# The last pair's MLP as two single visits, and matmuls without use while the visit pipeline fills

## The chip, the core and the metric

The kernel runs on one core of one Trainium2 chip. The core has five engines with queues of their own: TensorE (PE, with its weight loads shown apart as PEld), VectorE (DVE), ScalarE (ACT), GpSimd (POOL) and SyncE (SP), which here only starts DMAs. The metric is the device time in microseconds (us) of one execution, as the median of several runs.

## The reference

A batch of 8 sequences of 128 tokens with 144 channels goes through four layers.

```python
# layer 0: rotation in a subspace of 64 dimensions
U, _ = jnp.linalg.qr(P)                      # P is 144 x 64
R = expm(skew(silu(cond) @ W.T + b))         # one 64 x 64 rotation per sequence
z = einsum('btn,nd->btd', x, U)
x = x + einsum('btd,nd->btn', z @ R - z, U)
# layers 1 to 3: transformer blocks with modulation from cond, 16 heads of 9
h = norm(x) * (1 + scale_msa) + shift_msa
x = x + gate_msa * attention(h)              # softmax(q k^T / 3) v, then a projection
h = norm(x) * (1 + scale_mlp) + shift_mlp
x = x + gate_mlp * (gelu(h @ W_fc1 + b) @ W_fc2 + b)     # 144 -> 576 -> 144
```

The third block uses a root-mean-square norm and also normalises q and k; the first two use layer norm.

## The kernel before, in words

Until about 113 us the kernel builds the rotation (a QR by hand on DVE, the matrix exponential on PE) and loads all weights. `WARM_AT` (line 90, used in line 1066) puts 24 matmuls without use, of 512 columns each, between steps of the QR. `rotated` (line 1586) then adds the rotation to `x` in four parts on DVE.

From there on the work is cut into 24 *visits*: visit v is sequence v % 8 in block v // 8. A visit is normalised (`variances`, `normalise`, with the power -1/2 on POOL), its 16 last channels are split on POOL into bf16 parts (`tail_parts`, line 523, six small steps that wait for one another), it is transposed on PE (`h_turn`), scaled on ACT (`h_out`), multiplied with the qkv weights (`qkv`), split into bf16 parts (`first` on ACT, `split` on DVE), and transposed, half by PE (`parts_turn`) and half by two DMA transposes that SP starts (line 370). Then come the scores, their maxima on DVE (`maxima`, `max_parts`, `max_turn`, `max_out`), the scores again transposed, the exponentials, the product with v, the projection (`proj`), its gate (`gated`) and `attention_add` on POOL. `scores(v, 0)` takes heads that PE has transposed; `scores(v, 2)` waits for the DMA transposes.

The MLP runs in *pairs* of visits, m = v // 2, so 12 pairs: `second_input`, `second_deviation`, `second_normal`, `second_half_tail`, `h2_turn`, `h2_out`, `fc1` in three steps through PSUM banks 5, 0, 5, `gelu` after each step, `fc2` in two halves, `mlp_out` on DVE, `mlp_add` on POOL.

The order is written out by hand: every engine walks over the same slots (`for slot in range(-2, VISITS + 6)`) and each slot lists which visit or pair does what on that engine. `visit_at(work, v)` calls the work if v is a visit; `pair_at(work, slot, lag)` calls it for the pair m with slot = 2 m + lag. Even and odd slots differ, and in the third block some have an order of their own. Each engine works through its list strictly in order and waits at semaphores. `refill(bank, ...)` waits until the last reader of a PSUM bank is done. ACT must load a table to go between exp and gelu (`bring_table`); `to_exp` and `to_gelu` do that with an activation of one column. The last pair (m = 11, visits 22 and 23) has its norm in slot 25 and the rest of its MLP in slots 26 to 28, when there is no attention left. SP stores `x` in four transfers of two sequences, each after its pair's `mlp_add`.

Of the kernel before, what the change touches and what calls it, by code (L numbers as in the profile page):

```python
# [26 lines left out]
BF16 = mybir.dt.bfloat16  # L27
U32 = mybir.dt.uint32
I32 = mybir.dt.int32
ALU = mybir.AluOpType  # L30
# [3 lines left out]
B, T, C = 8, 128, 144  # L34
# [21 lines left out]
STEPS = LAYERS * B // 2  # L56
LN_EPS = [1e-6, 1e-5, 0.0]
# [6 lines left out]
VISITS = LAYERS * B  # L64

# [49 lines left out]
def program(nc, t, out, spread_mods):  # L115
    ctx = ExitStack()
    with ctx:
# [181 lines left out]
        fc2_full, mlp_ready, mlp_added = sem("fc2_full"), sem("mlp_ready"), sem("mlp_added")  # L299
        stored = sem("stored")  # L300
# [16 lines left out]
        def _(sp):  # L317
# [54 lines left out]
            for pair in range(B // 2):  # L372
                sp.wait_ge(mlp_added, STEPS - B // 2 + pair + 1)
                sp.dma_start(out[:, 2 * pair:2 * pair + 2, :], x[:, 2 * pair:2 * pair + 2, :]).then_inc(stored, 16)
            sp.wait_ge(stored, 16 * (B // 2))
# [3 lines left out]
        FC1_BANKS = (5, 0, 5)  # L379
        ROT_BANKS = (2, 4, 6, 2)  # L380

        def mlp_step(slot, lag):

            m = (slot - lag) // 2
            return m if slot >= lag and (slot - lag) % 2 == 0 and m < STEPS else None
# [6 lines left out]
        def pair_at(work, slot, lag, *args):  # L392

            if mlp_step(slot, lag) is not None:
                work(mlp_step(slot, lag), *args)
# [6 lines left out]
        def _(pool):  # L402
# [160 lines left out]

            def second_half_tail(m, h):
                second_tail(2 * m + h)
# [18 lines left out]
            for slot in range(-2, VISITS + 6):  # L584
                if (slot + 1) // B == 2 and slot % 2 == 0:
                    pair_at(second_half_tail, slot, 4, 1)
                    pair_at(mlp_add, slot, 6)
# [11 lines left out]
                elif slot % 2 == 0:  # L599
                    pair_at(second_half_tail, slot, 4, 1)  # L600
                    pair_at(mlp_add, slot, 6)
# [3 lines left out]
                else:  # L605
# [4 lines left out]
                    pair_at(second_half_tail, slot, 3, 0)  # L610


        @block.scalar
        def _(act):
# [161 lines left out]
            def to_exp(m):  # L776
                if m < STEPS - 1:
                    bring_table(ACT.Exp)
# [16 lines left out]
            def modulated(v, kind):  # L795

                h, l, b = v % 2, v // B, v % B
                out_, at = (hT_t[h][:], 0) if kind == 0 else (mT_t[:, h, :], h * T)
                return a.activation(out_, ps[:, 0, at:at + T], ACT.Identity, bias=mod_t[:, l, 2 * kind, b:b + 1],  # L799
                                    scale=mod_t[:, l, 2 * kind + 1, b:b + 1])  # L800

# [23 lines left out]
            for slot in range(-2, VISITS + 6):  # L825
# [49 lines left out]
                else:  # L875
# [11 lines left out]
                    visit_at(o_out, slot - 1)  # L887


        @block.tensor  # L890
        def _(pe):
# [276 lines left out]

            def parts_turn(v, k):
# [16 lines left out]
            def scores(v, g):  # L1186
                if g == 0:
# [62 lines left out]
            pe.wait_ge(sel_ready, 1)  # L1250
            h_turn(0)
            qkv(0)
            h_turn(1)
            for slot in range(-2, VISITS + 6):
# [60 lines left out]
                else:  # L1315
# [18 lines left out]
                    visit_at(pv, slot - 1, 3)  # L1334


        @block.vector
        def _(dve):
# [394 lines left out]

            def next_input(v):
# [35 lines left out]
            for slot in range(-2, VISITS + 6):  # L1770
                if (slot + 1) // B == 2 and slot % 2 == 0:
                    pair_at(mlp_out, slot, 6)
# [31 lines left out]
                elif slot % 2 == 0:  # L1804
                    pair_at(mlp_out, slot, 6)
# [12 lines left out]
                else:  # L1818
# [13 lines left out]
                    pair_at(second_normal, slot, 3)  # L1832

# [99 lines left out]
```

## Time and profile before

| | |
|---|---|
| median of 3 runs | 399.44 us (399.34 to 399.56) |
| profiled execution, its own time | 396.7 us |
| its span, first to last instruction | 394.9 us |
| busy: PE, DVE, ACT, POOL | 316.3, 297.9, 222.1, 165.1 us |
| chain that ended last | DVE 41%, PE 29%, issue 10%, ACT 6%, DMA 5%, POOL 5% |
| mean granted TensorE clock | 0.900 of full speed |

The profiled execution took 2.7 us less than the median. The page cuts the span into 40 slices of 9.87 us; digits are tenths. Granted clock 0.5 is 1.2 GHz, and 1.0 is 2.4 GHz. The chain is followed back from the last instruction; "issue" in it is time in which nothing that the profile shows was waited for.

### The profile page before, as it was taken

What the parts mean: (1) busy time and instruction counts of PE and PEld (TensorE: products, weight loads), DVE (VectorE), ACT (ScalarE), POOL (GpSimd) and SP (SyncE); (2) the same over time, 40 slices, a digit from 0 to 9 for tenths busy, and PEclk for the clock granted to TensorE, in tenths of its full rate; (3) what the DMA queues carried; (4) which work ended last, traced back from release to release, by engine and by line L of the source; (5) the groups of instructions that cost most, each with busy time, mean ns of one, the idle gap of its engine ahead of it and who ended that gap; (6) DMA issues with size and microseconds to landing.
All of it is one profiled execution on the core that took longest, in us unless ns stands there. A gap on an engine that the chain in (4) does not pass through costs nothing.

```text
span 394.9 us, 10842 instructions
## 1 busy us (share of the span) xinstructions
PE 316.3 (80%) x3516; PEld 215.9 (55%) x3516; DVE 297.9 (75%) x1507; ACT 222.1 (56%) x484; POOL 165.1 (42%) x536
## 2 busy tenths in 40 slices
PE   1979938836565678999999999988898888978935
PEld 1826413631232455777777776756566655756724
DVE  5999999999944778777777877768797888866110
ACT  3244101430023466879797978785868768575721
POOL 5434323656430313535444453535546364613140
PEclk9998556995765699999999999999999999999968
DMA  5797000194001221211121211110022111101000
GB/s 148 202 269 241 6 1 3 31 268 148 1 0 27 28 29 29 42 23 40 23 42 30 30 29 28 29 28 14 16 28 29 29 28 28 30 15 31 17 15 15
DMA packets 36303, 20.43 MB, mean 52 GB/s; under 512 B 27882, under 2 KB 34766, under 8 KB 36120
## 3 DMA queue, kind: packets, MB, share of 16 engines
q1 hardware_dynamic: 36248, 19.75, 21.0%
q8 instruction: 29, 0.48, 0.5%
q14 instruction: 26, 0.21, 0.2%
HBM read 12.82 MB, written 0.62 MB: 34 GB/s over the span
## 4 chain that ended last, share of the span: by engine, by line
DVE 41%; PE 29%; issue 10%; ACT 6%; DMA 5%; POOL 5%; SPq 2%; POOLq 0%; ACTq 0%; DVEq 0%
PE ps L893 23%; DMA skw_r<-brief 5%; DVE nmax L1683 4%; DVE grow L1380 4%; DVE top L1435 3%; DVE trow L1380 3%; DVE beta L1414 2%; DVE den L1420 2%; SPq L370 2%; PE ps L1173 2%; DVE tfac L1428 2%; PE ps L1234 2%; DVE brief L1670 2%; DVE lead L1402 2%; DVE late L1402 2%
## 5 line engine op out<-in xcount | busy, mean ns | idle before, releaser
L1683 DVE TENSOR_REDUCE nmax<-ps 128x4 f32<-128x512 f32 x96 | 62.3, 685 | 28.5 <-PE ps L893 28.3
L438 POOL TENSOR_TENSOR root<-grow,half 32x1 f32<-32x1 f32 x64 | 34.8, 544 | 53.2 <-DVE grow L1380 52.8
L754 ACT ACTIVATE skw_t<-ps 128x512 f32<-128x512 f32 x96 | 54.1, 596 | 5.2 <-PE ps L893 5.1
L893 PE MATMUL ps<-skw_r 54*128 54x128 bf16 x768 | 46.4, 222 | 7.1 <-DMA skw_r<-brief 4.5
L893 PEld LDWEIGHTS ps<-skw_r 54*128 54x128 bf16 x768 | 29.5, 96 | 21.4 <-issue 13.7
L893 PE MATMUL ps<-mT_t,fc1w_t 128*128 128x256 f32 x120 | 39.4, 421 | 2.0 <-ACT mT_t L799 1.6
L893 PE MATMUL ps<-fc2w,skw_r 128*128 128x144 f32 (+1 forms) x240 | 34.6, 292 | 0.6 <-ACT skw_r L786 0.6
L547 POOL TENSOR_TENSOR x<-x,skw_r 128x144 f32<-128x144 f32 x24 | 11.7, 489 | 53.5 <-DVE skw_r L1723 53.5
L893 PEld LDWEIGHTS ps<-fc2w,skw_r 128*128 128x128 f32 (+1 forms) x240 | 31.2, 190 | 3.9 <-issue 2.1
L552 POOL TENSOR_TENSOR rstd<-vare,nhalf 128x1 f32<-128x1 f32 x24 | 13.2, 552 | 45.5 <-DVE vare L1603 30.2
L771 ACT ACT_TABLE_LOAD x23 | 29.5, 1283 | 0.4
L893 PE MATMUL ps<-nmT,sel 64*128 64x128 bf16 x384 | 27.8, 219 | 0.0
L761 ACT ACTIVATE skw_t<-ps 128x512 f32<-128x512 f32 x24 | 14.3, 595 | 23.5 <-PE ps L893 23.5
L893 PE MATMUL ps<-skw_t,brief 128*32 128x128 f32 x512 | 22.1, 280 | 5.5 <-DVE skw_r L1723 4.9
L893 PE MATMUL ps<-qkvw_t,hT_t 128*128 128x432 f32 x48 | 24.9, 604 | 1.0 <-ACT hT_u L807 0.8
L893 PEld LDWEIGHTS ps<-mT_t,fc1w_t 128*128 128x128 f32 x120 | 19.2, 201 | 10.1 <-issue 7.0
L786 ACT ACTIVATE skw_r<-ps 128x512 f32<-128x512 f32 (+1 forms) x36 | 18.5, 522 | 8.7 <-PE ps L893 8.5
L1173 PE MATMUL ps<-identb,brief 128*128 128x128 bf16 x192 | 16.8, 226 | 8.0 <-DVE brief L1672 8.0
L538 POOL TENSOR_TENSOR tail<-ln,gmod 128x16 f32<-128x16 f32 x48 | 11.0, 228 | 25.7 <-DVE ln L1616 21.5
L747 ACT ACTIVATE skw_r<-ps 128x512 bf16<-128x512 bf16 x24 | 14.3, 595 | 9.6 <-PE ps L1173 9.1
L1173 PEld LDWEIGHTS ps<-identb,brief 128*128 128x128 bf16 x192 | 13.2, 101 | 11.4 <-issue 10.5
L893 PEld LDWEIGHTS ps<-nmT,sel 64*128 64x128 bf16 x384 | 19.0, 95 | 0.0
(262 smaller groups left out, 828.5 us busy)
## 6 DMA issues: line engine op xcount, KB each, us to landing
gmod<-spread_mods SPq DMA_DIRECT2D x3, 1408.0 KB, 13.2
adaw_t<-in_ada SPq DMA_DIRECT2D x3, 432.0 KB
tails<-in_tail SPq DMA_DIRECT2D x3, 427.1 KB
skw_t<-in_skw SPq DMA_DIRECT2D x1, 1024.0 KB
fc1w_t<-in_fc SPq DMA_DIRECT2D x3, 320.0 KB
fc2w<-in_fc SPq DMA_DIRECT2D x3, 288.0 KB
skw_r<-brief SPq DMA_TRANSPOSE x48, 2.6
qkvw_t<-in_qkv SPq DMA_DIRECT2D x3, 216.0 KB
```

The source lines that it names most:

```text
L438: g.tensor_tensor(root[:, p, j:j + 1], grow[:, i % 4, 0:1], half[:], ALU.pow).then_inc(root_ready, 1)
L552: g.tensor_tensor(rstd[:, 0, h:h + 1], vare[:, 0, h:h + 1], nhalf[:, 0:1], ALU.pow).then_inc(rstd1, 1)
L747: a.activation(qkT[1][v % 2][:, 0:4, :].rearrange("p k t -> p (k t)"), ps[:, 7, :].bitcast(BF16)[:, 0:4 * T], ACT.Copy).then_inc(kT_ready, 1)
L754: a.activation(prob[g].rearrange("p i t -> p (i t)"), ps[:, 2 + g % 2, :], ACT.Exp, scale=SCALE).then_inc(prob_ready, 1)
L761: a.activation(o_raw[v % 2].rearrange("p g t -> p (g t)"), ps[:, 4, :], ACT.Copy).then_inc(o_raw_ready, 1)
L771: a.activation(table_out[:], half[:], f).then_inc(table_used, 1)
L786: a.activation(hid[0:rows, 2 * r:2 * r + n, :, :].rearrange("p c h t -> p (c h t)"), ps[0:rows, FC1_BANKS[r], 0:n * 2 * T], f).then_inc(hi ...
L893: return pe.matmul(o, lhsT, rhs, start=start, stop=stop, skip_group_check=True)
L1173: i = pe.transpose(o[:, pair * T:(pair + 1) * T], parts[k][v % 2][:, 2 * pair:2 * pair + 2, :].rearrange("p h d -> p (h d)"), identb[:])
L1380: return d.stream_shuffle(out_, rows, [j] * HALF)
L1402: i = d.scalar_tensor_tensor(out=elim[p][:, w], in0=grow[:, (HALF * p + j) % 4, 1:D + 1], scalar=gfac[:, p, j:j + 1], in1=elim[p][:, w], o ...
L1683: d.tensor_reduce(nmax[:, v % 2, first:first + 7:2], ps[:, 6 + g % 2, :].rearrange("p (i t) -> p i t", i=4), AX_X, ALU.max, negate=True).t ...
```

## The change

It has two parts that don't touch.

*The end.* The MLP of visits 22 and 23 is no longer pair 11 but two single visits with functions `last_...`. There are 11 pairs left (`PAIRS`), the slots end at 25, and what the pair 10 would have done in slot 26 (`mlp_out`, `mlp_add`) is called by hand. Visit 22 is normalised in slot 24 on DVE and POOL, visit 23 after slot 25. On PE, after slot 25, come `last_turn(22)`, `last_tail_turn(22)`, `last_fc1_main(22)`, `last_fc1_tail(22)`, `last_turn(23)`, `last_products(22)`, and then visit 23's own steps. Each visit has four PSUM banks (`LAST_BANKS`), so neither waits for the other's. Matmuls of `fc1` now have 128 columns instead of 256, and all first parts of a visit stand ahead of all second parts. `to_exp` is left out after pair 10, and so is the next `to_gelu`. The last `x` addition is done on DVE instead of POOL, and SP stores the two last sequences one by one.

*The start.* `stay_warm(n)` issues n matmuls without use, of 512 columns in bf16, into PSUM bank 5. They stand in the PE list at: 4 before `h_turn(0)`, 6 inside it (between its two transposes), 4 after it, 1 after `qkv(0)`, 11 after `h_turn(1)`; then 6 ahead of `scores(0, 2)` and 6 ahead of `scores(1, 2)`, 6 ahead of `max_turn(0)` and 2 ahead of `max_turn(1)`: 46 in all.

```diff
+PAIRS = STEPS - 1
...
+LAST = VISITS - 2
...
-            for pair in range(B // 2):
+            for pair in range(B // 2 - 1):
                 sp.wait_ge(mlp_added, STEPS - B // 2 + pair + 1)
                 sp.dma_start(out[:, 2 * pair:2 * pair + 2, :], x[:, 2 * pair:2 * pair + 2, :]).then_inc(stored, 16)
-            sp.wait_ge(stored, 16 * (B // 2))
+            for b in range(B - 2, B):
+                sp.wait_ge(last_done, b - B + 3)
+                sp.dma_start(out[:, b:b + 1, :], x[:, b:b + 1, :]).then_inc(stored, 16)
+            sp.wait_ge(stored, 16 * (B // 2 + 1))
...
+        LAST_BANKS = ((1, 6, 7, 2), (0, 3, 4, 5))
...
-            return m if slot >= lag and (slot - lag) % 2 == 0 and m < STEPS else None
+            return m if slot >= lag and (slot - lag) % 2 == 0 and m < PAIRS else None
...
+            def last_deviation(v):
+                h = v % 2
+                pool.wait_ge(last_var, v - LAST + 1)
+                g.tensor_tensor(rstd[:, 1, h:h + 1], vare[:, 1, h:h + 1], nhalf[:, 0:1], ALU.pow).then_inc(last_rstd, 1)
+            def last_parts(v):
+                tail_parts(1, v, (last_ln, v - LAST + 1), (h2T_full, PAIRS), last_tail)
...
-            for slot in range(-2, VISITS + 6):
+            for slot in range(-2, VISITS + 2):
...
-                    pair_at(mlp_add, slot, 6)
+                    pair_at(mlp_add, slot, 6, stop=PAIRS - 1)
...
+                if slot == VISITS:
+                    last_deviation(LAST)
+                    last_parts(LAST)
+            last_deviation(LAST + 1)
+            last_parts(LAST + 1)
+            mlp_add(PAIRS - 1)
...
-                if m < STEPS - 1:
+                if m < PAIRS - 1:
...
+            def last_modulated(v):
+                act.wait_ge(last_turned, v - LAST + 1)
+                act.wait_ge(fc1_full, 3 * PAIRS)
+                modulated(v, 1, LAST_BANKS[v % 2][0], 0).then_inc(last_mod, 1)
+            def last_tail_out(v):
+                act.wait_ge(last_tail_turned, v - LAST + 1)
+                a.activation(mT_u[:, v % 2, :], ps[:, LAST_BANKS[v % 2][1], :].bitcast(BF16)[0:KS, 0:T],
+                             ACT.Copy).then_inc(last_u, 1)
+            def last_gelu(v, r):
+                act.wait_ge(last_fc1, 3 * (v - LAST) + r + 1)
+                act.wait_ge(fc2_full, PAIRS)
+                rows, n = (128, 2) if r < 2 else (64, 1)
+                bank = LAST_BANKS[v % 2][(2, 3, 0)[r]]
+                a.activation(hid[0:rows, 2 * r:2 * r + n, v % 2, :], ps[0:rows, bank, 0:n * T].rearrange("p (c t) -> p c t", t=T),
+                             ACT.Gelu_apprx_tanh).then_inc(last_hid, 1)
...
+            last_modulated(LAST)
+            last_tail_out(LAST)
+            last_gelu(LAST, 0)
+            last_gelu(LAST, 1)
+            last_gelu(LAST, 2)
+            last_modulated(LAST + 1)
+            last_tail_out(LAST + 1)
+            last_gelu(LAST + 1, 0)
+            last_gelu(LAST + 1, 1)
+            last_gelu(LAST + 1, 2)
...
+            def stay_warm(n):
+                for r in range(n):
+                    mm(ps[:, 5, :], identb[:], sel[:, 4 * (r % 4):4 * (r % 4) + 4, :])
...
                 pe.transpose(o[:, 0:T], ln[0][v % 2][:, 0:128], ident[:])
+                if v == 0:
+                    stay_warm(6)
                 pe.wait_ge(tailp_ready, v + 1)
...
+            def last_turn(v):
+                o = refill(LAST_BANKS[v % 2][0], last_mod, v - LAST + 1)
+                pe.wait_ge(v_ready, VISITS)
+                pe.wait_ge(last_ln, v - LAST + 1)
+                pe.transpose(o[:, 0:T], ln[1][v % 2][:, 0:128], ident[:]).then_inc(last_turned, 1)
+            def last_tail_turn(v):
+                o = refill(LAST_BANKS[v % 2][1], last_u, v - LAST + 1)
+                pe.wait_ge(last_tail, v - LAST + 1)
+                turn_parts(o.bitcast(BF16)[0:KS, 0:T], tailp[1][v % 2]).then_inc(last_tail_turned, 1)
+            def last_part(v, c):
+                bank, at = LAST_BANKS[v % 2][(2, 2, 3, 3, 0)[c]], (c % 2) * T
+                return ps[:, bank, at:at + T]
+            def last_fc1_main(v):
+                for bank in LAST_BANKS[v % 2][2:4]:
+                    refill(bank, last_hid, 3 * (v - LAST) + 2)
+                pe.wait_ge(last_mod, v - LAST + 1)
+                for c in range(FFC):
+                    mm(last_part(v, c), fc1w_t[2][:, c * 128:c * 128 + 128], mT_t[:, v % 2, :], c % 2 == 0, False)
+            def last_fc1_tail(v):
+                pe.wait_ge(last_u, v - LAST + 1)
+                for c in range(FFC):
+                    at = 3 * C + c * 128
+                    i = mm(last_part(v, c), tailw[:, 2, at:at + 128], mT_u[:, v % 2, :], False, True)
+                    if c % 2 == 1 or c == FFC - 1:
+                        i.then_inc(last_fc1, 1)
+            def last_products(v):
+                h = v % 2
+                for c in range(FFC):
+                    pe.wait_ge(last_hid, 3 * (v - LAST) + c // 2 + 1)
+                    rows = 128 if c < 4 else 65
+                    i = mm(ps[:, LAST_BANKS[h][1], 0:C], hid[0:rows, c, h, :], fc2w[2][0:rows, c, :], c == 0, c == FFC - 1)
+                i.then_inc(last_fc2, 1)
...
             def scores(v, g):
+                if v < 2:
+                    stay_warm(3 * g)
...
             def max_turn(v):
+                if v < 2:
+                    stay_warm(6 - 4 * v)
...
             pe.wait_ge(sel_ready, 1)
+            pe.wait_ge(rot_read, 2)
+            stay_warm(4)
             h_turn(0)
+            stay_warm(4)
             qkv(0)
+            stay_warm(1)
             h_turn(1)
-            for slot in range(-2, VISITS + 6):
+            stay_warm(11)
+            for slot in range(-2, VISITS + 2):
...
+            last_turn(LAST)
+            last_tail_turn(LAST)
+            last_fc1_main(LAST)
+            last_fc1_tail(LAST)
+            last_turn(LAST + 1)
+            last_products(LAST)
+            last_fc1_main(LAST + 1)
+            last_tail_turn(LAST + 1)
+            last_fc1_tail(LAST + 1)
+            last_products(LAST + 1)
...
+            def last_input(v):
+                dve.wait_ge(att_added, v + 1)
+                variances(1, [v], last_var)
+            def last_normal(v):
+                dve.wait_ge(last_rstd, v - LAST + 1)
+                dve.wait_ge(h2T_full, PAIRS)
+                normalise(1, v, last_ln)
+            def last_out(v):
+                h, b = v % 2, v % B
+                dve.wait_ge(last_fc2, v - LAST + 1)
+                dve.wait_ge(mlp_added, PAIRS)
+                need(did(d.tensor_tensor(mlpd[:, h, :], ps[:, LAST_BANKS[h][1], 0:C], gmod[:, 2, b, C:2 * C], ALU.mult)))
+                d.tensor_tensor(x[:, b, :], x[:, b, :], mlpd[:, h, :], ALU.add).then_inc(last_done, 1)
...
+                if slot == VISITS:
+                    last_input(LAST)
+                    last_normal(LAST)
+            last_input(LAST + 1)
+            mlp_out(PAIRS - 1)
+            last_normal(LAST + 1)
+            last_out(LAST)
+            last_out(LAST + 1)
```

## Rows read from the trace of the kernel before

**Rows 1.** The page: granted clock by slice of 9.87 us, in tenths.
```profile
PEclk9998556995765699999999999999999999999968
```
**Rows 2.** The chain, as pipeline fills: start us, us, what.
```profile
115.98 0.36 PE ps L1116
...
117.18 2.15 PE ps L893 x3
...
122.31 1.01 PE ps L1173 x8
123.32 2.49 PE ps L893 x11
...
127.24 0.63 PE ps L893 x8
...
131.40 1.19 SPq L370
...
132.63 3.31 DMA skw_r<-brief
```
**Rows 3.** By stretch: us, PE busy (instructions), PEclk, DMA share, GB/s.
```profile
114.00:115.00 1.00, 0.30 (x1) 0.83 0.00 0
...
134.00:135.00 1.00, 1.00 (x7) 0.50 0.32 58
```
**Rows 4.** Timeline of PE, the matmuls without use: start us, us, operation.
```profile
91.85 6.53 PE L893 MATMUL ps<-sel,identb 128*128 128x512 bf16 x15 [4.37 <-DVE grow L1380]
99.00 0.82 PE L893 MATMUL ps<-sel,identb 128*128 128x512 bf16 x3 [0.62 <-DVE grow L1380]
```
**Rows 5.** Timeline of PE later, at full clock: the filling's same groups.
```profile
148.98 0.61 PE L1173 MATMUL ps<-identb,brief 128*128 128x128 bf16 x8 [1.06 <-DVE brief L1672]
...
149.42 0.28 PE L1121 MATMUL ps<-ident,ln 128*128 128x128 f32 x1
...
150.95 0.99 PE L893 MATMUL ps<-qkvw_t,hT_t 128*128 128x432 f32 x2
...
151.78 0.35 PE L893 MATMUL ps<-tailw,hT_u 102*128 102x432 bf16 x1
```
**Rows 6.** Timeline, all engines, from the last attention work to the end.
```profile
373.84 1.39 PE L893 MATMUL ps<-fc2w,skw_r 128*128 128x144 f32 x10
...
374.43 0.49 POOL L547 TENSOR_TENSOR x<-x,skw_r 128x144 f32<-128x144 f32 x1 [7.58 <-DVE skw_r L1723]
...
377.53 0.22 POOL L538 TENSOR_TENSOR tail<-ln,gmod 128x16 f32<-128x16 f32 x1 [0.41 <-DVE ln L1619]
...
380.64 0.22 POOL L543 TENSOR_TENSOR tailp<-tail,tailp 128x16 bf16<-128x16 f32 x1
...
391.92 0.79 POOL L570 TENSOR_TENSOR x<-x,skw_r 128x288 f32<-128x288 f32 x1 [10.31 <-DVE skw_r L1731]
```
**Rows 7.** Timeline, one visit's norm alone, and visit 22's attention addition.
```profile
280.13 0.30 DVE L1597 BATCH_NORM_STATS2 st<-x 128x6 f32<-128x144 f32 x1
...
281.76 0.29 DVE L1619 TENSOR_SCALAR ln<-x,rstd 128x144 f32<-128x144 f32 x1 [0.67 <-POOL rstd L552]
...
366.35 0.49 POOL L547 TENSOR_TENSOR x<-x,skw_r 128x144 f32<-128x144 f32 x1
...
370.92 0.26 DVE L1708 RECIPROCAL orec<-ps 128x16 f32<-128x16 f32 x1 [4.70 <-PE ps L1234]
```
**Rows 8.** Timeline, prices of single steps near the end.
```profile
372.11 0.39 ACT L793 ACTIVATE x_t<-ps 128x256 f32<-128x256 f32 x1 [0.21 <-PE ps L1112]
...
374.04 0.31 DVE L1723 TENSOR_TENSOR skw_r<-ps,gmod 128x144 f32<-128x144 f32 x1 [2.52 <-PE ps L893]
...
381.57 0.80 ACT L799 ACTIVATE mT_t<-ps,mod_t 128x128 f32<-128x128 f32 x2
```
**Rows 9.** By stretch, near the end: us, PE busy (instructions), PEclk, DMA share, GB/s.
```profile
377.50:378.00 0.50, 0.40 (x2) 0.50 0.00 0
...
387.50:388.00 0.50, 0.50 (x3) 0.77 0.00 0
```

More of the change, by code:

```diff
@@ L299, in program @@
         fc2_full, mlp_ready, mlp_added = sem("fc2_full"), sem("mlp_ready"), sem("mlp_added")
+        last_var, last_rstd, last_ln, last_tail = sem("last_var"), sem("last_rstd"), sem("last_ln"), sem("last_tail")
+        last_turned, last_mod = sem("last_turned"), sem("last_mod")
+        last_tail_turned, last_u = sem("last_tail_turned"), sem("last_u")
+        last_fc1, last_hid, last_fc2, last_done = sem("last_fc1"), sem("last_hid"), sem("last_fc2"), sem("last_done")
         stored = sem("stored")
@@ L390, in visit_at, with pair_at @@
                 work(v, *args)
-        def pair_at(work, slot, lag, *args):
-            if mlp_step(slot, lag) is not None:
+        def pair_at(work, slot, lag, *args, stop=STEPS):
+            if mlp_step(slot, lag) is not None and mlp_step(slot, lag) < stop:
                 work(mlp_step(slot, lag), *args)
@@ L600, in _ @@
                     pair_at(second_half_tail, slot, 4, 1)
-                    pair_at(mlp_add, slot, 6)
+                    pair_at(mlp_add, slot, 6, stop=PAIRS - 1)
                     visit_at(attention_add, slot - 2)
@@ L793, in o_T, with modulated @@
                 a.activation(oT[v % 2].rearrange("p k t -> p (k t)"), ps[:, 4, 0:2 * T], ACT.Copy).then_inc(oT_ready, 1)
-            def modulated(v, kind):
+            def modulated(v, kind, bank=0, at=None):
                 h, l, b = v % 2, v // B, v % B
-                out_, at = (hT_t[h][:], 0) if kind == 0 else (mT_t[:, h, :], h * T)
-                return a.activation(out_, ps[:, 0, at:at + T], ACT.Identity, bias=mod_t[:, l, 2 * kind, b:b + 1],
+                out_ = hT_t[h][:] if kind == 0 else mT_t[:, h, :]
+                at = h * T * kind if at is None else at
+                return a.activation(out_, ps[:, bank, at:at + T], ACT.Identity, bias=mod_t[:, l, 2 * kind, b:b + 1],
                                     scale=mod_t[:, l, 2 * kind + 1, b:b + 1])
+            def last_modulated(v):
[13 more added lines that the diff above has]
+                             ACT.Gelu_apprx_tanh).then_inc(last_hid, 1)
             def h_out(v):
@@ L1250, in _ @@
             pe.wait_ge(sel_ready, 1)
+            pe.wait_ge(rot_read, 2)
+            stay_warm(4)
             h_turn(0)
+            stay_warm(4)
             qkv(0)
+            stay_warm(1)
             h_turn(1)
-            for slot in range(-2, VISITS + 6):
+            stay_warm(11)
+            for slot in range(-2, VISITS + 2):
                 if (slot + 1) // B == 2 and slot % 2 == 0:
@@ L1768, in second_normal @@
                     normalise(1, v, ln2_ready)
-            for slot in range(-2, VISITS + 6):
+            for slot in range(-2, VISITS + 2):
                 if (slot + 1) // B == 2 and slot % 2 == 0:
-                    pair_at(mlp_out, slot, 6)
+                    pair_at(mlp_out, slot, 6, stop=PAIRS - 1)
                     visit_at(q_out, slot)
@@ L1804, in _ @@
                 elif slot % 2 == 0:
-                    pair_at(mlp_out, slot, 6)
+                    pair_at(mlp_out, slot, 6, stop=PAIRS - 1)
                     visit_at(attended, slot - 2)
```

## The prediction

> **What bounds the kernel now.** First the page: the granted clock by slices shows two stretches of the visit part at less than full speed, the filling of the pipeline after about 113 us and the last three slices [rows 1]. The change touches just these. So two views were read for each: the chain of waits, which says what ends last, and the timeline with the table by stretch, which say what a step costs at either clock.
>
> In the filling no engine is full; the chain goes from one engine to the next: norm, transposes, qkv, split, scores, maxima. Its TensorE pieces are 0.36, 2.15, 1.01, 2.49 and 0.63 us [rows 2], all at 0.5 of the clock: it fell in the microsecond after 114 and was still 0.5 in the one before 135 [rows 3]. Behind that stretch the chain waits for a DMA transpose, 1.19 us on SP and 3.31 us to its landing [rows 2], so what comes later moves rigidly with the start of that DMA.
>
> At the end, attention is over when `attention_add` of visit 23 ends at 374.92 (374.43 + 0.49) [rows 6]. Then the last pair's MLP runs alone: norm of both visits, two bf16 splits on POOL one after the other (377.53 to 380.86), transposes, scaling, fc1, gelu, fc2, gate and the last addition, which ends at 392.71 [rows 6]. That is 17.8 us in which nearly nothing overlaps. The span ends at 394.9, so 2.2 us more for the last store.
>
> **The end, part by part.** Visit 22's attention is added at 366.84 (366.35 + 0.49) [rows 7], 8 us before visit 23's. A single visit's norm takes 1.92 us from its statistics to the end of the normalised tile (280.13 to 282.05) [rows 7]; a split of one visit takes half of 3.33, so 1.7 us [rows 6]. Visit 22 in slot 24 is thus normalised by 368.8 and split by 370.6. I cost it at nothing: TensorE is in pair 10's fc1, attention's end and fc2 until 375.23 (373.84 + 1.39) [rows 6]. The waits that this adds in slot 24: on DVE the next item, `attended(23)`, stands behind `last_normal(22)` and ran at 370.92 [rows 7], 2.1 us after it; on POOL `attention_add(23)` stands behind the split and ran at 374.43, 3.9 us after. Were that cover gone, a late split would push everything after 374.43 one for one.
>
> From 375.23 on, the path in steps; durations are at full clock:
> - transpose of 22: 0.28 [rows 5], ends 375.5; scaling on ACT, half of the 0.80 for two visits [rows 8] and some fixed part, so 0.46: 376.0; with 0.1 for the hand-over 376.1.
> - `last_fc1_main(22)`: no row has f32 matmuls of 128 columns. Nearest are fc2's of 144 columns, ten in 1.39 us [rows 6], so 0.26 to 0.28 for the two records of a chunk. Five chunks are 1.3: 377.4. Bounds: 1.1, and 2.4 at half clock by the ratio below.
> - second parts and the first gelu: 0.4 until ACT begins, 377.8. Two gelus of 256 columns at 0.39 (the copy of that size) [rows 8] and one of 128 columns, taken as 0.3: 378.9. Meanwhile visit 23 has been normalised (374.92 + 1.92 = 376.9) and `last_turn(23)` done; `last_products(22)` follows the gelus and ends at about 379.4.
> - scaling of 23, which ACT has behind 22's gelus: 0.46 and hand-over, 379.4. Five chunks: 380.8. Visit 23's split is done at 378.7, hidden. Its transpose and the copy by ACT stand behind the main part: 0.7, 381.5. Second parts: 381.9. Gelus: 383.0. Last product: 0.5, 383.5.
> - gate 0.31 [rows 8] and the same for the addition on DVE: 384.2.
>
> The last addition ended at 392.71, so this part gives 8.5 us. The table loads that go lay beside POOL's splits and TensorE's first fc1 steps and give nothing. `mlp_add(10)` moves behind the split of 23, to about 379.5, and holds up `last_out(22)` on DVE; the next item there, `last_out(23)`, comes at 383.5, so it costs nothing. SP stores one sequence last instead of two; I take the 2.2 us as before. Bounds of the part: 9.5 if ACT and hand-overs are shorter than taken, 4.8 if all of it ran at half clock (the rival below).
>
> **The start, part by part.** A matmul without use costs 0.435 us at half clock (15 in 6.53), and three issued at once later took 0.82 with the last one's latency in it, which fits 0.22 each [rows 4]. That the clock rises under them is in the same rows. If it stays full from 114 on:
> - the 4 before `h_turn(0)` end at about 114.4, just when its transpose can run. The 6 inside end at about 116.0, when POOL's split ends (115.98 is when the next transpose began) [rows 2]. The 4 after it take 0.9 beside ACT's scaling (116.34 to 117.18). Cost nothing to 0.1.
> - `qkv(0)`: 2.15 becomes 1.18 (150.95 to 152.13) [rows 2, 5]: 1.0 gained.
> - 1 + 11 run beside the split into parts on ACT and DVE, which takes 3.0 us (119.33 to 122.31) [rows 2]; they end about 0.15 after the parts are ready: 0.15 lost.
> - `parts_turn` 1.01 to 0.61 [rows 2, 5], `qkv(1)` 2.15 to 1.18, scores 0.63 to 0.43: 1.5 gained, so maxima start 2.4 earlier. Then `scores(0, 2)` follows them, but it needs the DMA transposes as well. By the chain's own pair, 1.19 + 3.31, they land up to 4.5 after the parts; they would be 0 to 0.5 later than DVE. I take 0.2 lost, the last scores give 0.2 back.
> - the 6 ahead of `scores(0, 2)` and 6 ahead of `max_turn(0)` are 1.3 each, beside maxima that take 1.4 (125.81 to 127.24) [rows 2]: nothing. The 6 ahead of `scores(1, 2)` end with the DMA they wait for: 0.1. The 2 ahead of `max_turn(1)`: 0.43 us of work where TensorE has little time free, 0.15 taken. After that the clock was full before too, so nothing more.
>
> Sum: 1.0 − 0.15 + 1.5 − 0.1 and − 0.4 for small collisions is about 1.8 us. Bounds: 2.6, and −1 if parts of it run at half clock.
>
> **The sum.** 8.5 + 1.8 = 10.3. The profiled execution would go from 396.7 to 386.4, its span from 394.9 to 384.6. The median shown is 2.7 above that execution; I subtract the gain from it: 399.44 − 10.3 = 389.1 us.
>
> **Rivals.**
> - *Clock falls at 114.8 all the same.* Before, TensorE was busy for 0.30 of the microsecond after 114, and the clock fell in it [rows 3]; the change adds four matmuls, 0.9 us, just before. If it falls, the 6 inside `h_turn(0)` take 2.6 instead of 1.3 and hold the second transpose 1.3 back, the 4 after it some 0.4 more, until the added work has raised the clock again; of the later gains what is left leaves about 0.4 for the start: 390.5. For it: that fall. Against it: six more follow almost at once.
> - *Clock falls in the tail.* Ratio 2.15 to 1.18 [rows 2, 5]. All of it at half: each main part of fc1 +1.0, `last_products(22)` +1.2 before TensorE is free for 23, the rest +0.5: 3.7 lost, 392.8; half of it, 391.0. Against: before, TensorE had nothing to do from 375.23 and was at 0.5 only in the stretch from 377.50 [rows 9]; now the hole is 0.6 to 0.9 us. The same row shows the price before: clock back only in the stretch from 387.50.
> - Beside it, a rule: the Trainium skill (TensorE: Matmul & The Clock Gate, Part 4: PE-mode transpose) says that transposes do not count as work for the clock as matmuls do. By that rule the transposes at 375.2 would not help, and this second rival, 391.0, would be likelier; no row here separates the two.
> - *The added matmuls stand in the way (slower).* If the clock does not rise under them, all 46 cost 0.435, not 0.22. By the places above, in half-clock lengths (six are 2.6 from 115.6 on where the transpose wants to start at 116.0, and so on): 2.2 + 0.8 in `h_turn(0)` and behind it, 2.8 for the 11, 1.1, 0.4, 2.4 for the three sixes, 0.5 for the two: 10.2 lost against 8.5 won, 401.1. It decides from 8.5 us on. Against it: [rows 4] show the clock raised by just such matmuls.
> - *The single visits do not overlap as said*, for instance since ACT holds visit 23 back behind 22's gelus for longer: half of the end's gain, 393.4.
>
> **How the numbers follow.** Forecast 389.1: 62%. Fall at 114.8, 390.5: 17%. Fall in the tail, 391.0: 12%. No overlap, 393.4: 5%. Slower, 401.1: 2%. Something in between with no change: 2%. The range reaches up over the tail rival to 392.4, and down by the upper bounds of both parts, 9.5 and 2.6, to 387.3. About 0.2% is what can be told from no change here. Faster 0.96, within 0.02, slower 0.02.
>
> **What would show it.** Right: granted clock near 1.0 without a break from 111 us on; `qkv(0)` at 1.2 us; `last_turn(22)` directly behind the last `fc2`; last addition on DVE about 9.3 us after `attention_add(23)` ends, instead of 17.8. The start is read from where the first DMA transposes of visit 1 begin: 131.40 before, 129.3 to 129.7 after. Wrong: a stretch at 0.5 in either place, fc1 chunks of 128 columns well above 0.28, a transpose or `scores(0, 2)` waiting behind added matmuls, `attended(23)` or `attention_add(23)` late behind visit 22's new steps.

## The result, and the profile after

The changed kernel takes 386.33 us (median of 4; 384.53 to 386.86), against 399.39 for the kernel before: ratio 0.9695, interval 0.9653 to 0.9737. The gain is 13.1 us; the forecast was 10.3, and 386.33 lies under the range's lower end of 387.3. But the profiled executions fell only from 396.7 to 386.9, by 9.8 us. That sum looks nearly right, but the table says otherwise. It cuts the span at the first rotated addition on DVE and at the attention additions on POOL, which this text numbers from 1 to 24 (the 24th is visit 23's). It gives what each stage gained, once from the first profile to the changed kernel's first, and once between the means of three profiles of each kernel (*before*, *e1* and *e16* against *after*, *e4* and *e15*; the runs are told below).

| stage | forecast | first pair, us | means of three, us |
|---|---|---|---|
| start of the span to the first rotated addition | 0 | -0.72 | -0.25 |
| from there to the 4th addition (the filling) | 1.8 | -0.34 | 1.71 (62.29 to 60.58) |
| 4th to 11th addition | 0 | 0.01 | -0.11 |
| 11th to 14th addition | 0 | 1.88 | 1.86 (31.96 to 30.10) |
| 14th to 24th addition | 0 | 0.02 | 0.02 |
| end of the 24th to the end of the last addition | 8.5 | 8.81 | 8.74 (17.72 to 8.98) |
| last addition to the end of the span | 0 | 0.14 | 0.17 |
| sum | 10.3 | 9.8 | 12.1 |

So in the first pair the forecast's 1.8 us of the filling did not come, and 1.9 us came from a stage that the forecast had as rigid. In the later runs, 85 executions of the kernel before spread from 396.1 to 402.0 us, with their median at 398.4: the same code differs by several us from one execution to the next.

The page's clock row of the changed kernel (slices of 9.63 us, tenths), to be held against [rows 1]:

```profile
PEclk9988555568969898999999999999999999999999
```

The last slices are full, and the filling (from the thirteenth slice on) nearly so; the twelfth slice, which ends at 115.5 us, has 0.6. The end, from the timeline of the changed kernel (start us, us, engine, operation):

```profile
372.99 1.39 PE L946 MATMUL ps<-fc2w,skw_r 128*128 128x144 f32 x10
...
373.58 0.49 POOL L557 TENSOR_TENSOR x<-x,skw_r 128x144 f32<-128x144 f32 x1 [3.81 <-DVE skw_r L1840]
...
374.22 0.27 PE L1233 MATMUL ps<-ident,ln 128*128 128x128 f32 x1
...
375.13 1.35 PE L946 MATMUL ps<-mT_t,fc1w_t 128*128 128x128 f32 x10 [0.58 <-ACT mT_t L824]
...
376.63 0.81 ACT L842 ACTIVATE skw_r<-ps 128x256 f32<-128x256 f32 x3 [1.48 <-PE ps L946]
...
378.40 1.28 PE L946 MATMUL ps<-mT_t,fc1w_t 128*128 128x128 f32 x10
...
380.86 1.49 PE L946 MATMUL ps<-fc2w,skw_r 128*128 128x144 f32 x10 [0.31 <-ACT skw_r L842]
...
382.74 0.31 DVE L1866 TENSOR_TENSOR x<-x,skw_r 128x144 f32<-128x144 f32 x1
```

From the end of `attention_add(23)` (374.07) to the last addition (383.05) it is 8.98 us, against 17.79 in [rows 6]. The transpose of visit 22 stands directly behind fc2, and the five chunks of fc1 take 1.35 us for one visit and 1.28 us for the other.

The filling, from the changed kernel's chain (start us, us, what) and its table by stretch (us, PE busy (instructions), PEclk, DMA share, GB/s):

```profile
116.97 2.01 PE ps L946 x7
...
129.88 0.61 PE ps L1271 x8
...
131.27 5.21 PE ps L946 x41
```

```profile
113.00:114.00 1.00, 1.00 (x8) 0.50 0.00 0
114.00:115.00 1.00, 0.74 (x6) 0.94 0.00 0
...
128.00:129.00 1.00, 0.22 (x1) 1.00 0.00 0
129.00:130.00 1.00, 0.12 (x3) 1.00 0.00 0
...
131.00:132.00 1.00, 0.96 (x17) 0.59 0.62 126
132.00:133.00 1.00, 1.00 (x2) 0.50 0.64 131
```

Where [rows 2] had 2.15, 1.01 and 2.49 us, the pieces are shorter, and the parts of visit 1 are ready 17.1 us after the first rotated addition began instead of 19.5. (The 2.01 us hold four of the added matmuls beside `qkv(0)`.) But the clock is not full throughout. It is at half until 114 us. TensorE has almost nothing to do from 127.6 to 129.9, the clock falls in the microsecond after 131, and now 5.21 us of TensorE stand on the chain where the DMA transposes stood [rows 2]. In them are `qkv(2)` and the six matmuls ahead of `scores(1, 2)`, both at half clock:

```profile
131.81 1.81 PE L946 MATMUL ps<-qkvw_t,hT_t 128*128 128x432 f32 x2
133.41 0.57 PE L946 MATMUL ps<-tailw,hT_u 102*128 102x432 bf16 x1
133.77 1.87 PE L946 MATMUL ps<-sel,identb 128*128 128x512 bf16 x6
```

### The profile page after: what moved, and what is told of

Read it like the earlier page. It is cut to its first block, busy times and chain, and to the rows that moved or that the text cites. A ratio compares the mean times of both kernels' runs of the same rounds, so it can differ in the third digit from the quotient of the medians.

```text
span 385.1 us, 10978 instructions
## 1 busy us (share of the span) xinstructions
PE 327.4 (85%) x3577; PEld 222.2 (58%) x3577; DVE 299.3 (78%) x1511; ACT 218.8 (57%) x484; POOL 165.2 (43%) x536
## 4 chain that ended last, share of the span: by engine, by line
DVE 41%; PE 39%; ACT 7%; issue 5%; DMA 3%; POOL 3%; SPq 1%; ACTq 0%; DVEq 0%
PE ps L946 31%; DVE grow L1497 4%; DVE nmax L1800 4%; DVE top L1552 3%; DVE trow L1497 3%; DMA skw_r<-brief 3%; DVE beta L1531 2%; PE ps L1336 2%; PE ps L1271 2%; DVE den L1537 2%; DVE tfac L1545 2%; DVE lead L1519 2%; DVE late L1519 2%; DVE brief L1787 1%; ACT L795 1%
## 5 line engine op out<-in xcount | busy, mean ns | idle before, releaser
L946 PE MATMUL ps<-mT_t,fc1w_t 128*128 128x256 f32 (+1 forms) x130 | 36.6, 381 | 1.4 <-ACT mT_t L824 0.9
L562 POOL TENSOR_TENSOR rstd<-vare,nhalf 128x1 f32<-128x1 f32 x24 | 13.3, 553 | 42.5 <-DVE vare L1720 27.5
L946 PE MATMUL ps<-sel,identb 128*128 128x512 bf16 x70 | 19.8, 412 | 5.7 <-DVE grow L1497 5.4
L946 PE MATMUL ps<-qkvw_t,hT_t 128*128 128x432 f32 x48 | 24.0, 584 | 0.2 <-issue 0.2
L1271 PE MATMUL ps<-identb,brief 128*128 128x128 bf16 x192 | 15.9, 219 | 5.4 <-DVE brief L1789 5.4
L810 ACT ACTIVATE skw_r<-ps 128x512 f32<-128x512 f32 (+1 forms) x33 | 16.9, 521 | 5.7 <-PE ps L946 5.5
L946 PEld LDWEIGHTS ps<-skw_t,brief 128*32 128x32 f32 x512 | 11.6, 108 | 12.9 <-DVE skw_r L1840 5.8
```

What stands on the lines that cost most here:

```text
L562: g.tensor_tensor(rstd[:, 0, h:h + 1], vare[:, 0, h:h + 1], nhalf[:, 0:1], ALU.pow).then_inc(rstd1, 1)
L810: a.activation(hid[0:rows, 2 * r:2 * r + n, :, :].rearrange("p c h t -> p (c h t)"), ps[0:rows, FC1_BANKS[r], 0:n * 2 * T], f).then_inc(hi ...
L946: return pe.matmul(o, lhsT, rhs, start=start, stop=stop, skip_group_check=True)
L1271: i = pe.transpose(o[:, pair * T:(pair + 1) * T], parts[k][v % 2][:, 2 * pair:2 * pair + 2, :].rearrange("p h d -> p (h d)"), identb[:])
```

## The experiments

"Gain" is against the executions of the kernel before on the same chip.

**Each part alone.** *e1* is the kernel before unchanged; *e2* has only the start's matmuls, *e3* only the end; *e4* is the changed kernel again. The edit of e3 in the changed kernel (the added wait on `rot_read` goes too; e2 is the reverse on the kernel before):

```diff
             def stay_warm(n):
-                for r in range(n):
+                for r in range(0):
```

> The kernel before, unchanged, profiled once more. The first profiled execution (396.7 us, mean clock 0.900) lay 2.7 us under the median 399.4. Theory A (what varies from execution to execution is how long the clock stays at half in the filling and in the tail, the two stretches that the change touches): this profile lies near 399 with a mean clock under 0.90, and its extra time stands between 113 and 135 us or after 375 us; the work before 113 us lasts as long within 0.3 us. Theory B (it varies in the rotation part, before the first visit, as the 0.72 us between the starts of the visits in the two profiles suggests): the time from the addition of the first rotated part to the end stays at 283 us within 0.5, and the extra stands before it.

> Only the matmuls without use are added to the kernel before; the last pair's MLP stays a pair. Profiles of before and after put the start at 1.6 us, from the first rotated part to the end of visit 23's attention (262.2 to 260.6 us from addition to addition). Theory A: against the median the start is worth more, 3 to 4.5 us, since a usual execution of the kernel before loses more in the filling than the profiled one did. Theory B: 1.3 to 2 us. The prediction's own term was 1.8.

> Only the single visits at the end; no matmul without use in the filling. The profiles put the end at 8.8 us (17.8 to 9.0 from the end of visit 23's attention addition to the last addition). Theory A, with the variation in the filling: 8.5 to 9.3 against the median. Theory A, with the variation in the tail: 11 to 12, and then the start alone is worth 1.6. Theory B: 8.5 to 9.3, and start and end don't add up to the 13.1 that both together gave.

> The changed kernel once more, on the chip and beside the same runs of the kernel before as the other three. If gains add up, its gain is the sum of those of the start alone and of the end alone within 0.7 us; it was 13.1 at first. A gain near 10.3 would mean that the first comparison was off; a gain of 13 with parts of 1.6 and 8.8 would mean that the two parts help one another, for which I have no mechanism.

Measured: e1 397.78 us, ratio 0.9978 (0.9951 to 1.0005); e2 395.45, 0.9902 (0.9867 to 0.9938); e3 388.75, 0.9745 (0.9718 to 0.9771); e4 385.61, 0.9668 (0.9641 to 0.9696). By the ratios, the gains of e2, e3 and e4 are 3.9, 10.2 and 13.3 us of 399.3. The two parts make 14.1 together, 0.8 more than both at once, just outside the 0.7 expected; the intervals are wide enough for that, so they add up as far as can be told. Each is worth more than its forecast term, 1.8 and 8.5, and e3's 10.2 lies outside all that was expected of it. The unchanged e1 came out 0.2% under its own kernel, so a ratio near 0.998 is no gain. The tail, from visit 23's attention addition to the last addition, took 17.94 us in e1, 17.93 in e2, 8.98 in e3 and 8.99 in e4. In the other profiles with the old tail it was 17.43 (e16), 17.28 (e9) and 16.80 (e13), never longer, and in all but e8 of those with the new one about 9.0. So the variation that would have made the end worth 11 to 12 us (the second reading of theory A in e3) is out.

The profile of e1 (399.94 us) shows what the first one did not. Chain and stretches of e1:

```profile
141.43 4.07 DMA skw_r<-brief
```

```profile
144.00:145.00 1.00, 0.00 (x0) 1.00 0.07 8
145.00:146.00 1.00, 0.41 (x8) 0.77 0.02 8
...
148.00:149.00 1.00, 0.45 (x6) 0.50 0.00 0
...
152.00:153.00 1.00, 1.00 (x15) 0.82 0.64 131
```

A DMA transpose of visit 2 landed in 4.07 us instead of 3.34 in the first profile; TensorE waited, and the clock fell a second time, for 7 us. From the first to the fourth attention addition e1 took 31.6 us, the first profile 28.5. So theory A is right that the clock makes the difference, but not about the place, which is neither before 135 us nor in the tail. Theory B is out, since e1's first rotated addition began only 0.3 us later than the first profile's.

**A third look at the kernel before**, e16, a single execution:

> A third profile of the kernel before. Theory A: if its time is near 399 it has a second fall of the clock between 144 and 153 us, or its first return is later than 136 us, and the stretch from the first to the fourth attention addition is above 30 us; if its time is near 397 it has neither, and 28.5 us.

It took 398.76 us, with 30.5 us from the first to the fourth addition, the same late landing and the second fall:

```profile
142.29 4.08 DMA skw_r<-brief
```

```profile
147.00:148.00 1.00, 1.00 (x28) 0.54 0.00 0
148.00:149.00 1.00, 0.77 (x13) 0.50 0.00 0
...
153.00:154.00 1.00, 1.00 (x11) 0.54 0.61 123
```

That is as theory A said for this profile. Two of three profiles of the kernel before have the second fall; the one that the forecast rested on has not. Taking the fall away, e13:

```diff
             def scores(v, g):
+                if (v, g) == (2, 2):
+                    stay_warm(4)
             def max_turn(v):
+                if v == 2:
+                    stay_warm(3)
             def parts_turn(v, k):
+                if (v, k) == (3, 0):
+                    stay_warm(4)
```

> The kernel before with 11 matmuls without use in visits 2 and 3 only (4 ahead of scores(2, 2), 3 ahead of max_turn(2), 4 ahead of parts_turn(3)), where one of two profiled executions had a second stretch at half clock (146 to 152 us) and took 3 us more by it. Theory A (a usual execution of the kernel before has that second fall, and the first profile was one of the lucky ones): the median falls by 1 to 2.5 us against the kernel before beside it, and the profile shows the clock full from 136 us on. If the fall is rare: 0 to 0.5 us.

397.63 us, ratio 0.9974 (0.9939 to 1.0009), 0.7 us under the kernel before beside it: less than expected, and no more than the unchanged e1 showed. In its profile the second fall is gone (28.6 us for the first four additions), but the clock came back from the first stretch only at 141 us, not 135. Its stretch from the 11th to the 14th addition was 30.1 us too, like that of the changed kernel (below). Its twelve executions still spread from 394.8 to 400.3 us. So how much of the median's excess over the first profile is the second fall stays open; that it is in the two slower profiles is seen.

**The single visits.** In *e8* visit 22 is normalised and split after slot 25:

```diff
-                if slot == VISITS:
-                    last_input(LAST)
-                    last_normal(LAST)
+            last_input(LAST)
+            last_normal(LAST)
             last_input(LAST + 1)
```

(and the same on POOL).

> The changed kernel, but visit 22's norm and split are done after slot 25, directly ahead of visit 23's, and no longer in slot 24. The prediction's reading: the norm then starts at 374.1 instead of 366, its transposes wait for the split, 3.6 us instead of none after fc2, and visit 23's split comes behind; the tail from attention addition to last addition grows from 9.0 to about 11.5 to 13 us, the more if the clock falls in the hole. So of the 8.8 us about 3 are from doing visit 22 early and 5 to 6 from shorter steps and overlap of the two. Rival: the steps after the norms set the time anyway; under 1.5 us longer.

389.77 us, 0.9782 (0.9735 to 0.9828); the tail took 12.53 us. So 3.55 of the 8.8 us come from doing visit 22 early. The other 5.3 us, shorter steps, overlap of the two visits and a clock that in the kernel before was at half from 377.5 to 387.5 us [rows 9], were not taken apart. Part of the 3.55 is the clock too (e8):

```profile
373.00:374.00 1.00, 0.00 (x0) 1.00 0.00 0
374.00:375.00 1.00, 0.30 (x1) 1.00 0.00 0
375.00:376.00 1.00, 0.23 (x2) 0.70 0.00 0
376.00:377.00 1.00, 1.00 (x6) 0.50 0.00 0
```

```profile
375.97 2.47 PE L945 MATMUL ps<-mT_t,fc1w_t 128*128 128x128 f32 x10
```

With only two transposes in 3 us the clock fell, and fc1 of one visit took 2.47 instead of 1.35 us. In the changed kernel the hole is 0.6 us and it did not.

**The holes in the filling.** *e5* leaves out the six ahead of `scores(1, 2)`; *e6* puts them behind `max_turn(0)`; *e7* adds 3 ahead of `max_turn(2)` and 4 ahead of `parts_turn(3)`. The edit of e6:

```diff
             def scores(v, g):
-                if v < 2:
+                if v < 1:
                     stay_warm(3 * g)
...
                 pe.transpose(o[:, 0:T], nmp[v % 2][:], identb[:]).then_inc(mT_full, 1)
+                if v == 0:
+                    stay_warm(6)
```

> The changed kernel without the 6 matmuls ahead of scores(1, 2). In both profiles of the changed kernel the clock fell at about 132 us and those 6 then took 1.7 to 1.9 us on the chain, so that scores(1, 2) ran about 1 us after its DMA transposes could have let it. Theory P (they stand in the way): time from the first rotated addition to the last scores of visit 1 falls by 0.8 to 1.2 us, the time falls by 0.5 to 1.2 us. Theory Q (they are what brings the clock back at 135): without them it comes back one stretch later, and the time is the same or up to 1.5 us longer.

> The same 6 matmuls moved to the place directly behind max_turn(0), where TensorE has nothing to do for 1.6 us before parts_turn(1). If the fall at 132 comes from the hole between 127.6 and 130.5 us, the clock now stays full there, and visit 1 is through by about 1.5 to 2 us earlier than in the changed kernel: 384.0 to 384.8 where the changed kernel has 385.7. If the hole is not the cause, the fall stays and the gain is at most that of leaving the 6 out.

> As the kernel with the moved six, and in addition 3 matmuls ahead of max_turn(2) and 4 ahead of parts_turn(3), into the holes between 146 and 148.6 us in front of the second fall (149.4 to 152.6 us) of the changed kernel. If that fall costs time, this gains another 0.5 to 1.5 us (383 to 384 us) and the executions lie closer together than the 1.5 us between lowest and highest of the changed kernel; if the chain there is made by DMA and VectorE, the clock stays full and the time does not change.

e5: 385.51 us, 0.9697 (0.9644 to 0.975); e6: 383.6, 0.9621 (0.9586 to 0.9656); e7: 383.48, 0.9631 (0.9591 to 0.9671). Leaving the six out gains nothing in the time: in e5 the clock fell all the same, at 130 us. Moved into the hole they bring about 2 us. The 7 matmuls that e7 adds to that bring nothing more, so the changed kernel's own second fall of the clock (148 to 151 us in its first profile) costs no time that shows. Chain and stretches of e6:

```profile
130.57 2.50 DMA skw_r<-brief
133.07 0.09 issue
133.16 0.89 PE ps L946 x24
```

```profile
128.00:129.00 1.00, 1.00 (x6) 1.00 0.00 0
...
131.00:132.00 1.00, 0.93 (x10) 1.00 0.31 63
132.00:133.00 1.00, 0.46 (x2) 1.00 0.51 102
```

The clock stays full and the DMA is on the chain again. But one profile of each does not show that the hole makes the fall: with the six in their old place the clock fell at 131 or 132 us in the profiles of *after* and e4, and stayed full past 140 us in those of e2, e8, e11 and e15, behind about the same hole. From the first rotated addition to the third exponential of visit 0 (line 778), the first step of ScalarE on the chain behind that place, it is 23.9 and 25.0 us in *after* and e4, 22.4 to 23.2 in the four without the fall, and 21.8 with the moved six (e6). So e6 is 0.5 us or more ahead even where the clock did not fall, and 2 to 3 us where it did. On one chip with the changed kernel once more:

> The kernel with the moved six, beside the changed kernel on one chip. It was 3.8% below the kernel before, where the changed kernel was 3.1 to 3.3% below. If the hole behind max_turn(0) is what costs the changed kernel 1 to 2 us: again 1 to 2 us under it, ratio 0.963 to 0.966. If the difference was one between chips: equal.

> The changed kernel again, beside the moved six: ratio 0.967 to 0.970.

e14: 383.97 us, 0.9651 (0.9609 to 0.9693); e15: 385.41, 0.9679 (0.9637 to 0.9722). Over all runs the moved six have 383.7 us (12) and the changed kernel 385.6 (16). I take the moved six as the better kernel by 1 to 2 us, though the intervals on the one chip overlap.

The profile of e7 (386.87 us) caught an execution in which the clock came up late, at 118 us, and so did that of e14 (386.9 us):

```profile
117.00:118.00 1.00, 1.00 (x4) 0.51 0.00 0
```

```profile
114.50 1.87 PE L946 MATMUL ps<-sel,identb 128*128 128x512 bf16 x4 [0.26 <-DVE x L1711]
116.17 0.42 PE L1179 MATMUL ps<-ident,ln 128*128 128x128 f32 x1
116.38 2.26 PE L946 MATMUL ps<-sel,identb 128*128 128x512 bf16 x6
118.47 0.22 PE L1169 MATMUL ps<-identb,tailp 128*102 128x128 bf16 x1
```

There the added matmuls did stand in the way: visit 0's parts were ready 10.7 us after the first rotated addition began (10.8 in e14), not 9.2, and later than the 10.2 of the kernel before. *e12* tried to bridge the hole before 105.7 us, with `WARM_AT = range(54, 63)` in e6's kernel:

> The kernel with the moved six (383.6), and three more matmuls without use behind the 62nd step of the QR, into the hole before 105.7 us where the clock falls and from which it is at half through the rotation's last products (2.8 us of them on the chain) and in some executions into the filling. If the clock stays full: these products take 0.8 to 1.3 us less, the executions in which it rises late (one took 386.9) go away, and the median is 382.3 to 383. If it falls nevertheless: 383.6 with the same spread. Six more instructions move the loads little.

385.79 us, 0.9697 (0.9658 to 0.9735): the clock fell at 105.9 all the same, and the time is about 2 us longer than with the moved six alone, not equal as expected. Its profile is of its fastest execution (383.7 us) and shows no reason; this stays open.

**Two microseconds far from both parts.** In each profile I took the time from the 11th to the 14th attention addition on POOL. It is 32.0, 32.1 and 31.8 us in the three profiles of the kernel before and 32.2 in e3, but 30.1 in e2, e4 and the changed kernel, whose code there is that of the kernel before. On the chain of e3, two of TensorE's waits stand out; this is the second:

```profile
253.13 1.20 SPq L376
254.37 4.30 DMA skw_r<-brief
```

Elsewhere such transposes land in 2.5 us. Two other transfers ran beside it, one load of instructions on queue q8 and one on q14 (the page has 29 and 26 of them in the span). That q8 is TensorE's is inferred: it is the loads of q8 that the next edits move. *e9* to *e11* shift TensorE's instructions against the work. The edit, with n = 46 (e9, on the kernel before; e10, on e3) or 82 (e11, on the changed kernel):

```diff
             pe.wait_ge(sel_ready, 1)
+            for i in range(n):
+                mm(ps[0:32, 3, 0:4], identb[:, 0:32], sel[:, 0, 0:4])
             for i in WARM_AT:
```

> The kernel before plus 46 matmuls of 4 columns in TensorE's idle time at 88 us, well before the visits: as many TensorE instructions as the change adds at the start (92 with the weight loads), with no effect on the clock in the filling. Theory S: TensorE's instructions are loaded in pieces of 16 KB (29 such loads), and where a load meets the DMA transposes of a visit, these land in 4.0 to 4.4 us instead of 2.5; 92 more instructions move the loads. Then the stretch from the 11th to the 14th attention addition falls from 32.0-32.2 to 30.1 us, as in all kernels that have the start's matmuls, and the time by about 2 us, to 396.7. Theory F: the 2 us come from the faster filling; then the stretch stays at 32 and the time at 398.7.

> The same 46 small matmuls in the kernel with the single visits alone (388.75). Theory S: 386.7, so that the start's matmuls are left with only 1 us of the 3 us between 388.75 and 385.7. Theory F: 388.7.

> The changed kernel plus 82 small matmuls at the same early place: together with the change's 46 that is 256 instructions or one 16 KB piece, so the loads stand again where they stood in the kernel before. Theory S: the stretch from the 11th to the 14th addition goes back to 32 us and the time to about 387.6. Theory F: 385.7, 30.1.

The stretch was 30.1 us in e9, 30.1 in e10, and back at 31.95 in e11, as theory S has it. Over all twenty profiles it is 30.85 to 32.2 us in the five with no instruction added to TensorE ahead of it, 30.1 in the fourteen with 22 (e13) to 106 (e7), and 31.95 with 256 (e11). The transposes of that place, three in the window taken of e10, two of e3 and four of e11:

```profile
DMA to landing us min/median/max: 2.4/2.6/3.1
```

```profile
DMA to landing us min/median/max: 3.1/3.7/4.3
```

```profile
DMA to landing us min/median/max: 2.5/2.8/4.0
```

What differs is the load beside them. The DMA view of that place has both of these lines in the kernel before (253 to 258 us, landing 4.37), and only the second in e9 (252 to 257 us):

```profile
q8 instruction: 1, 0.02, 1.1%
q14 instruction: 1, 0.01, 0.4%
```

On the chains of the twenty profiles there are 24 landings of more than 3.6 us, and a q8 load runs beside every one; beside the 58 shorter ones it runs 3 times. The landings behind which the clock fell in e1 and e16, 4.07 and 4.08 us, are among the 24, and the first profile's 3.34 is not. That is a close tie, though nobody moved a load and nothing else.

In the times: e9 397.24 us, 0.9976 (0.9948 to 1.0003); e10 387.48, 0.9751 (0.9713 to 0.9789); e11 387.5, 0.9715 (0.9679 to 0.9751), 1.9 and 2.1 us above e4 and e15. Only e11's came as expected. e9's ratio is that of the unchanged e1, and e10's is that of e3 (0.9745). One pair more, on one chip:

> The single visits alone once more, beside the same with 46 small early matmuls on one chip: 0.9745 of the kernel before as at first, and 32 us from the 11th to the 14th attention addition.

> If the placement of the instruction loads is worth 2 us of device time, and not only of one profile: 1.5 to 2 us under e17_end_again, and 30.1 us from the 11th to the 14th addition. The first comparison stood across two chips and showed none (0.9751 against 0.9745). If again equal, the small matmuls give back elsewhere what they bring at that place.

e17: 388.68 us, 0.9764 (0.9726 to 0.9803); e18: 387.59, 0.9723 (0.969 to 0.9756), 1.1 us less. The stretch was 30.85 and 30.1. So the late landing itself varies from execution to execution (32.2 in e3, 30.85 in e17, of the same code). That the place of the instructions decides this stretch is shown in the profiles; in the time the four comparisons give 0 to 2 us, and none is clear of its interval.

## Why the prediction was wrong, point by point

- *"What comes later moves rigidly with the start of that DMA"*: the failed step that weighs most, a term put at nothing. Between the 11th and 14th additions 1.9 us were gained, in the first pair of profiles as in the means of three. They go with TensorE's instruction count, through the landing of one or two DMA transposes. The late landings were in the trace: the chain had one of 4.00 us and one of 4.37 there.
- *"I subtract the gain from it"* (the sum): the second failed step. The gain was read from one execution and taken off a median 2.7 us above it, as if these 2.7 were a constant. They are work that the executions differ in. The filling, from the first rotated addition to the 4th attention addition, took 60.7 us in the first profile and 63.4 and 62.7 in e1 and e16 (399.9 and 398.8 us), which have the second fall of the clock. The changed kernel can have that fall too, but it costs it less: 61.1, 60.8 and 59.9 us there in its three profiles. Against the first profile the start is thus worth -0.3 to 0.9 us, and against the mean of three 1.7. From e1 to *after* the gain of the profiles is 13.1, as measured, but e1 is the slowest of the three profiles of the kernel before; the means of three give 12.1. Of the 2.8 us by which the forecast was short, 1.9 are the step above and 0.4 the end; the rest is of the size by which executions differ, and stays open.
- *The start, 1.8 us*: right in the means (1.7), and by luck, since it was worked out against an execution faster than usual and for a clock that stays full. It did not: it was at half until 114 us, and in *after* and e4 fell again at 131 or 132. Up to visit 1's parts the change gives 2.4 us in its first profile (19.5 to 17.1), 2.4 in e2 and 1.4 in e4. Then in *after* the fall at 131, which I had excluded ("the clock was full before too, so nothing more"), and six matmuls at 1.87 instead of 1.3 take it back. I priced each added group by what waits for it, but never looked at what is left empty between the groups. With the same code in the filling, the eight profiles without the added matmuls took 60.4 to 63.4 us (mean 61.6), and the six with them 58.0 to 61.1 (mean 59.6). e2's 3.9 us have the 1.9 of the place of the instructions in them.
- *The end, 8.5 us*: right in mechanism and size, 8.8 in the profile (17.79 to 8.98). The chunks at 1.3 (1.35 and 1.28), the start directly behind fc2, and no delay of `attended(23)` or `attention_add(23)` all held. The 2.2 us behind the last addition became 2.05. In time the end alone gained 10.2 (e3) and 9.4 (e17); the 0.6 to 1.4 above the profile's figure is not explained by a step that I can name.
- *Rivals.* The fall at 114.8 is not in the changed kernel's profile; its nearest kin is the late rise in e7 and e14, 1.5 us. The fall in the tail did not come, but e8 shows it, at the price of 1.1 us for one visit's fc1. In e8 two transposes in 3 us did not hold the clock. The rule of the Trainium skill (TensorE: Matmul & The Clock Gate, Part 4) that transposes do not count for it is not contradicted by that, but no run had enough of them to tell that apart from plain idleness. The slower case did not come: the clock is full under the added matmuls from 115 us on, though in e7 and e14 only from 118, and there the start gave nothing up to visit 1's parts (19.8 and 20.1 us against 19.5). The single visits overlapped as said.

## What to carry to other kernels

Before a profile's gain is taken off a median, ask what a usual execution has that the profiled one has not; two or three profiles of the kernel before would have shown here a second fall of the clock, 2 to 3 us in the profiles that have it, and landings that move about. Matmuls without use belong into the holes: six of them brought nothing ahead of a waiting product (385.6 us with them, 385.5 without) and 2 us in the hole before it (383.7). And where one late transfer decides, a change far away can move a stage by 2 us, here with nothing but the place of the instructions in TensorE's stream: before a gain is put down to a change, compare the stages that it does not touch.

## What was not expected of the hardware

- A DMA transpose that lands in 2.5 us alone took 4.0 to 4.7 in some visits, each time with a load on the instruction queue q8 beside it; adding 46 early matmuls with no other use took it away at one place (4.30 to at most 3.1), and filling up to 256 added instructions brought it back (4.0).
- The granted clock fell at different moments in executions of the same code: its first return in the filling came at 135 us in the first profile of the kernel before, at 137 in the third after a short rise at 127, and with 46 early small matmuls at 138 (e18) without that rise.
